# Tokens of experts 1 to 3: sixteen-bit halves transposed by DMA in place of TensorE transposes

## What is computed

```python
logits = flat_x @ Wg + bg                       # 2048 tokens, E = 4 experts
top_vals, top_idx = jax.lax.top_k(logits, 2)
probs = softmax(logits where chosen, -inf elsewhere)
for i in range(E):
    score = jnp.where(assigned, probs[:, i], -jnp.inf)
    sel_p, sel_idx = jax.lax.top_k(score, 512)  # capacity
    tok = flat_x[sel_idx]                       # 512 x 512
    h = jax.nn.gelu(tok @ W1[i])                # 512 x 2048
    y = h @ W2[i] * p                           # 512 x 512
    out = out.at[sel_idx].add(y)
```

## Time and profile before

| | |
|---|---|
| median of 3 runs | 478.77 us (478.63 to 479.13) |
| the profiled execution | 477.77 us, its span 476.0 us |
| mean granted clock of TensorE | 0.957 of full speed |
| busy PE, DVE, ACT, POOL | 414.5, 292.1, 313.1, 108.0 us |

### The profile page before, as it was taken

How to read it: one execution, slowest core, us unless ns; L and a number is a source line. 1 busy time by engine, 2 the same in 40 slices (tenths; PEclk the granted TensorE clock), 3 DMA queues, 4 the chain that set the end, 5 groups by cost and what they waited for, 6 DMA issues and landing times.

```text
span 476.0 us, 7146 instructions
## 1 busy us (share of the span) xinstructions
PE 414.5 (87%) x2039; PEld 201.4 (42%) x2039; DVE 292.1 (61%) x596; ACT 313.1 (66%) x487; POOL 108.0 (23%) x126
## 2 busy tenths in 40 slices
PE   2586877712899999999999999999999999999991
PEld 2343343401554444454444444444444444444440
DVE  7999999988499976564674155457514635560000
ACT  6798888998669773926778780577879147760000
POOL 0787746701300002521001311100041110001111
PEclk9999998955699999999999999999999999999997
DMA  7994120499400828438001925600092310001211
GB/s 265 341 351 180 44 90 1 161 343 360 129 2 0 349 91 291 109 74 326 0 0 61 372 52 196 204 0 1 11 374 79 42 24 0 0 0 9 36 22 22
DMA packets 23126, 59.64 MB, mean 125 GB/s; under 512 B 1280, under 2 KB 1408, under 8 KB 21056
## 3 DMA queue, kind: packets, MB, share of 16 engines
q1 hardware_dynamic: 19008, 50.17, 28.5%
q0 software_dynamic: 3664, 8.65, 9.0%
q10 hardware_dynamic: 432, 0.54, 0.3%
HBM read 46.78 MB, written 12.58 MB: 125 GB/s over the span
## 4 chain that ended last, share of the span: by engine, by line
PE 74%; DVE 15%; issue 3%; ACT 2%; POOL 2%; DMA 1%; ACTq 0%; DVEq 0%; POOLq 0%
PE ps L818 35%; PE ps L803 26%; PE ps L781 7%; DVE arena L1280 6%; PE ps L744 2%; DVE arena L1299 2%; DVE arena L1310 2%; PE ps L714 1%; DVE arena L1536 1%; DMA arena<-xn_table,idx 1%; PE ps L610 1%; ACT early L883 1%; POOL arena L1139 1%; PE ps L736 1%; DVE arena L1658 0%
## 5 line engine op out<-in xcount | busy, mean ns | idle before, releaser
L818 PE MATMUL ps<-arena 128*128 128x512 f16 x768 | 167.7, 379 | 0.0
L803 PE MATMUL ps<-arena,early 128*128 128x512 f16 x576 | 124.8, 379 | 0.0
L818 PEld LDWEIGHTS ps<-arena 128*128 128x128 f16 x768 | 74.6, 98 | 88.1
L803 PEld LDWEIGHTS ps<-arena,early 128*128 x576 | 56.3, 98 | 68.0
L1046 ACT ACTIVATE arena<-ps,up 128x512 f32<-128x512 f32 x64 | 43.8, 684 | 58.6 <-PE ps L803 40.0
L1709 DVE SCALAR_TENSOR_TENSOR arena<-arena,h_down 128x512 f32 x48 | 36.1, 751 | 58.9 <-ACT arena L1049 58.9
L1218 POOL DMA_INDIRECT result<-arena,idx x16 | 27.6, 1724 | 191.0 <-DVE arena L1737 137.8
L1049 ACT ACTIVATE arena<-arena,h_down 128x512 f32 x64 | 46.2, 721 | 8.7 <-ACT arena L1046 0.2
L1689 DVE SCALAR_TENSOR_TENSOR early<-w_raw,down,early 128x2048 f16<-128x2048 f32 x16 | 37.1, 2346 | 18.9 <-ACT early L1007 18.8
L1737 DVE TENSOR_SCALAR arena<-ps,yscale 128x512 f32<-128x512 f32 x16 | 12.0, 748 | 59.1 <-PE ps L818 49.1
L1052 ACT ACTIVATE arena<-rows,down x64 | 45.2, 706 | 0.0
(11 more groups left out here) (226 smaller groups left out, 461.2 us busy)
## 6 DMA issues: line engine op xcount, KB each, us to landing
w_raw<-in_L_ffn_W SPq DMA_DIRECT2D x4, 4096.0 KB, 13.9
rows<-in_L_ffn_W SPq DMA_DIRECT2D x3, 4096.0 KB, 17.6
rows<-in_L_ffn_W SPq DMA_DIRECT2D x4, 1024.0 KB, 9.2
result<-rows SPq DMA_DIRECT2D x3, 1024.0 KB, 6.8
early<-in_ctx SPq DMA_DIRECT2D x2, 1024.0 KB, 6.3
rows<-in_x SPq DMA_DIRECT2D x2, 1024.0 KB, 11.0
xn_table<-arena SPq DMA_DIRECT2D x4, 512.0 KB, 5.2
xn_table<-arena SPq DMA_DIRECT2D x2, 1024.0 KB, 4.8
```

The source lines that it names most:

```text
L803: last = nc.tensor.matmul(ps[:, PH[q], :], w[:, k, at], t[:, k, :], start=n == 0, stop=n == 3 * CT - 1)
L818: last = nc.tensor.matmul(ps[:, PY[s % 2], :], h[:, t, s * P:(s + 1) * P], w[:, t, :], start=t == 0 and n == 0, stop=t == HT - 1 and n == 2)
```

## The change

For experts 1 to 3 the tokens are split before they are transposed. ACT writes the high halves of a gathered piece as rows into a new buffer `tok_rows_hi` (which lies where `hot` lies). DVE writes the low halves as rows over the gathered piece itself (`tok_rows_lo` is a 16-bit view of `tok`). SP then issues, for each expert, four DMA transposes of 128 x 512 16-bit elements for the high and four for the low halves, from SBUF to SBUF, into `tok_hi` and `tok_lo`. A new semaphore, `c_across`, counts them (16 each). The up product of expert e waits for all eight of its own; so do the next `hot` table on DVE and the next gather on POOL.

```diff
+        tok_rows_lo = tok[:, :, :].rearrange("p s d -> p (s d)").bitcast(F16).rearrange("p (s d) -> p s d", s=ST)[:, :, 0:D]
+        tok_rows_hi = part(arena, [at[0]], (ST, D), F16)
...
-            with sp.Fori(1, E) as e:
+            for e in range(1, E):
...
+                for s in range(ST):
+                    sp.wait_ge(c_tokhi, START + e * CT + s + 1)
+                    sp.dma_start_transpose(tok_hi[:, :, s * P:(s + 1) * P], tok_rows_hi[:, s, :]).then_inc(c_across, 16)
+                for s in range(ST):
+                    sp.wait_ge(c_toklo, START + e * CT + s + 1)
+                    sp.dma_start_transpose(tok_lo[:, :, s * P:(s + 1) * P], tok_rows_lo[:, s, :]).then_inc(c_across, 16)
...
-                for k in blocks:
-                    for s in range(ST):
-                        last = nc.tensor.transpose(ps[:, PT[k], s * P:(s + 1) * P], tok[:, s, k * P:(k + 1) * P], ident)
-                    last.then_inc(c_tokt, 1)
...
                 pe.wait_ge(c_w1hi, START + (e + 1) * CT)
+                pe.wait_ge(c_across, e * 2 * ST * 16)
...
-                            if q == 0:
-                                pe.wait_ge(c_tokhi, START + e * CT + k + 1)
-                                pe.wait_ge(c_toklo, START + e * CT + k + 1)
...
-                down_block(e, 0)
-                down_block(e, 1)
-                tokens(e + 1, (0, 1))
-                down_block(e, 2)
-                tokens(e + 1, (2, 3))
-                down_block(e, 3)
+                for s in range(ST):
+                    down_block(e, s)
...
-            down_block(0, 3, {5: lambda: tokens(1, range(CT))})
+            down_block(0, 3)
...
+            def high_rows(done):
+
+                for s in range(ST):
+                    act.wait_ge(c_tok[s], (done + 1) * 16)
+                    hold(act, "act")
+                    nc.scalar.copy(tok_rows_hi[:, s, :], tok[:, s, :]).then_inc(c_tokhi, 1)
...
                 w1_high(e + 1)
+                high_rows(e + 1)
                 w2_magnitudes(e + 1)
-                token_high(e + 1)
...
-                pool.wait_ge(c_tokt, START + (e + 1) * CT)
+                if e == 0:
+                    pool.wait_ge(c_tokt, START + CT)
+                else:
+                    pool.wait_ge(c_across, e * 2 * ST * 16)
...
+            def token_low(done):
+
+                for s in range(ST):
+                    dve.wait_ge(c_tokhi, START + done * CT + s + 1)
+                    nc.vector.tensor_tensor(tok_rows_lo[:, s, :], tok[:, s, :], tok_rows_hi[:, s, :], ALU.subtract).then_inc(c_toklo, 1)
...
             take_y(0, 2)
-            w1_low(1, (2,))
-            token_low(1, range(CT))
-            w1_low(1, (3,))
+            token_low(1)
+            w1_low(1, (2, 3))
...
                 take_y(e, 1)
-                token_low(e + 1, (0, 1))
+                token_low(e + 1)
                 w1_low(e + 1, (2, 3))
                 take_y(e, 2)
-                token_low(e + 1, (2, 3))
```

More of the change, by code:

```diff
@@ L381, in program @@
         b_shift = sem("shifted_ready")
-        b_rsum = sem("softmax_sum_ready")
         b_wide = sem("wide_probs_ready")
@@ L417, in program @@
         c_none = sem("unneeded_rows_landed")
-        c_zero = sem("unneeded_index_set")
         c_tokt = sem("tokens_transposed")
@@ L421, in program @@
         c_toklo = sem("token_lo_ready")
+        c_across = sem("token_halves_transposed")
         c_wtop = sem("weight_top_ready")
@@ L430, in program @@
         c_wpow2 = sem("weight_power_bounded")
-        c_wpow3 = sem("weight_power_inverted")
         c_down = sem("weight_scale_ready")
@@ L549, in _ @@
             first_w2(3, (4,))
-            with sp.Fori(1, E) as e:
+            for e in range(1, E):
                 sp.wait_ge(c_w1hi, START + e * CT)
                 sp.wait_ge(c_w1lo, START + e * CT)
-                sp.dma_start(w1_raw[:, :, :], w1_v[:, bass.ds(e, 1)].rearrange("p a k h -> p (a k) h")).then_inc(s_w1, 16)
+                sp.dma_start(w1_raw[:, :, :], w1_v[:, e]).then_inc(s_w1, 16)
                 sp.wait_ge(c_w2hi, START + e * HT)
                 sp.wait_ge(c_w2lo, START + e * HT)
-                sp.dma_start(w2_raw[:, :, :], w2_v[:, bass.ds(e, 1)].rearrange("p a t d -> p (a t) d")).then_inc(s_w2, 16)
+                sp.dma_start(w2_raw[:, :, :], w2_v[:, e]).then_inc(s_w2, 16)
+                for s in range(ST):
[4 more added lines that the diff above has]
+                    sp.dma_start_transpose(tok_lo[:, :, s * P:(s + 1) * P], tok_rows_lo[:, s, :]).then_inc(c_across, 16)
         @block.tensor
@@ L704, in next_list @@
                 last.then_inc(b_hotused, 1)
-            def tokens(done, blocks):
-                for s in range(ST):
-                    pe.wait_ge(c_tok[s], (done + 1) * 16)
-                pe.wait_ge(b_taken, done * 2 + 2)
-                for k in blocks:
-                    for s in range(ST):
-                        last = nc.tensor.transpose(ps[:, PT[k], s * P:(s + 1) * P], tok[:, s, k * P:(k + 1) * P], ident)
-                    last.then_inc(c_tokt, 1)
             def keep_warm(count):
@@ L1039, in gelu_and_w2 @@
                 act.wait_ge(c_hsc, START + 2 * e + 2)
+                hold(act, "act")
+                act.wait_ge(c_w2sum, START + e * CT + CT)
                 hold(act, "act")
@@ L1230, in _ @@
                 pool.wait_ge(s_x1st[g], 16)
-            nc.gpsimd.memset(none[:, :], 0).then_inc(c_zero, 1)
-            pool.wait_ge(c_zero, 1)
+            nc.gpsimd.memset(none[:, :], 0).then_inc(s_mhalf, 1)
+            pool.wait_ge(s_mhalf, 3)
             nc.gpsimd.indirect_dma_start(tok[:, ST - 1, :], None, xn2_table, bass.IndirectOffsetOnAxis(ap=none[:, 0:1], axis=0),
@@ L1452, in _ @@
             step(nc.vector.tensor_reduce(psum_r[:, :], pex[:, :, :], AX.X, ALU.add))
-            nc.vector.reciprocal(psum_r[:, :], psum_r[:, :]).then_inc(b_rsum, 1)
-            dve.wait_ge(b_rsum, 1)
+            step(nc.vector.reciprocal(psum_r[:, :], psum_r[:, :]))
             for n in range(2):
@@ L1482, in scales_of @@
                 dve.wait_ge(c_wpow2, START + count)
-                nc.vector.tensor_copy(up[:, m:m + 1], wpow[:, m:m + 1]).then_inc(c_wpow3, 1)
+                nc.vector.tensor_copy(up[:, m:m + 1], wpow[:, m:m + 1])
                 nc.vector.reciprocal(down[:, m:m + 1], wpow[:, m:m + 1]).then_inc(c_down, 1)
@@ L1804, in _ @@
                 halves_of_h_and_w2(e, 0, 2)
+                dve.wait_ge(c_across, e * 2 * ST * 16)
+                hold(dve, "dve")
                 slots(e + 1)
```

## The result

The changed kernel takes 473.12 us in the median of 6 runs (472.65 to 475.01), beside 478.70 us for the kernel before (6 runs, 477.75 to 479.13). The ratio is 0.989, with a 95% interval of 0.987 to 0.991. The sum of the prediction gave 473.5 us.

The account below looks back on a forecast made before the run. TensorE's solid chain was taken to bound the kernel; removing 48 transposes takes off 5.23 us, with the DMA transposes hidden at no cost: 478.77 - 5.23 = 473.54 us on the median. The range was 472.5 to 491 us.

Parts of the forecast that it names:

- Which engine bounds: From 205 to 466.26 us the chain is TensorE alone, so a microsecond leaving TensorE there leaves the time.
- The size of the gain: Taking 48 transposes off TensorE's chain, 1.75 + 4 x 0.87 us, gains 5.23 us at most.
- When the rows are ready: Expert 1's high rows from ACT ready at 196.8 to 200.7 us, low ones from DVE at 202.7 to 204.9.
- The price c: Time by which one DMA transpose follows another in a train on SP's queue: 1.36 us.
- The landing of the last: Expert 1's last transpose, started at 206.8 us, lands 3.9 us later at 210.7, 0.8 us ahead of need.
- nothing exposed: The new wait before the up products costs nothing, hidden by down block 3; hidden or under 1.5 us exposed, chance 0.57.
- The third: Rival: each 128x128 block in a transfer pays on its own, c 5.3 us or more; about 549 us, chance 0.13.
- the first two rivals: Ahead of up products: partly hidden, 474.8 to 476.5 us, chance 0.13; transposes one after another, 490 or 507 us, chance 0.12.
- the clock's part: After a long stall TensorE's granted clock drops to 0.50 and recovers, losing 1.3 us.
- a pace of 2.5 us: Second rival's deciding point: expert 1 5.3 us late, experts 2 and 3 in time, no change; around it, chance 0.05.
- What was costed at nothing: Dropped up product waits, SP's written-out loop and regrouped semaphores sit where nothing is late: zero; transposes' new wait hidden: nothing.
- ACT's later magnitudes: On ACT, W2's magnitudes end 4 to 5 us later, at 208.2 us, before DVE wants them at 209.5: nothing shifts.

Follow-up runs that it names:

- the wide transposes: Changed kernel with an expert's four high transposes of 128 x 512 made two of 128 x 1024, low ones unchanged: 472.91 us, 0.988 of the kernel before.
- the late train: Changed kernel, but SP waits for all four low pieces of an expert before issuing the first of its eight transposes: 482.78 us, 1.010 of before.
- the small edits: Kernel before with only the SP loop written out and three semaphores dropped or regrouped: 478.61 us beside 478.05, ratio 1.0007.
- the halved transposes: Changed kernel with each DMA transpose cut into two of 128 x 256 elements, 16 for an expert: 489.35 us, 1.024 of before.

## Why the prediction was right

**Which engine bounds.** Right, and shown: what leaves TensorE's chain leaves the time, and what is added to it is added to the time (doubled transposes, 5.6 us).

**The size of the gain.** 5.23 us forecast, 5.6 measured in the medians (an interval of 4.2 to 6.0), 5.24 in the two traces on the stretch that the change touches. The traces are the firmer check: 5.6 and 5.23 differ by less than the interval.

**When the rows are ready.** Within 0.9 us: the first high rows at 197.5 (forecast: 196.8, in a profile that ran 0.94 us later), the fourth low piece at 205.3 (204.9). ACT's copies were 0.62 us long rather than 0.72, DVE's four from SBUF 2.48 us, as from PSUM, where I had allowed 2.9. That the transfers would have the DMA engines almost to themselves held only in part: in 276 to 284 us of expert 2 their share was 0.49, but in 200 to 210 us of expert 1 it was 0.82 to 1.24.

**The price c.** 1.36 us was taken from the gathers on POOL's queue; 1.3 was measured. The number was right by luck: I took it as the pace of independent transfers, from the gathers' issue on POOL, and it is the issue of a transposing instruction on SP, the same for 64 to 256 KB, while a load costs SP 0.37 us. The landing of the last, 3.9 us forecast, was 2.6, with 5.0 and 3.9 just ahead of it. So expert 1 had 2.1 us of room in place of 0.8, or 1.4 with the 0.75 us from the landing to the first matmul, which the forecast left out. The term that counted, nothing exposed, was right; it was right by 1.4 us.

**The rivals.** None of them took place. The third, a price for each 128x128 block, is ruled out by size: two, four and eight blocks take 1.24, 1.26 and 1.3 us. The Trainium skill's 1309 ns in "VectorE: DVE Perf Modes", "The three transpose paths", is for one block of 128x128. No run here has a transpose of one block alone, but instructions of two, four and eight blocks take no more than that of the queue, so multiplying it by the blocks gave a price that these runs don't bear out. By the 261 GB/s of the Trainium skill's page "DMA: Bandwidth & Descriptors", "Latency and other measured facts", a transpose would take 0.5 us by estimate. The pace was 1.3 us, set by the issue, and in the windows of the wide transposes the engines, with shares of 0.96 and 1.12, moved 181 and 211 GB/s, a fifth to a third less. What I held against the change besides, that a transpose costs TensorE only 0.109 us, did not count: it is 0.109 us of the engine that bounds the time, against 1.3 us for each transfer on a queue and on engines that had room. The place of the first two rivals was right, as the trains made longer show: the wait ahead of the up product is where a late train appears, first on expert 1. Their price per stall was too low. I put the clock's part at 1.3 us; it was 1.8 to 2.6 us after stalls of 2.8 us and more (and 0.2 us after those of 1.6 us and less). So at a pace of 2.5 us the change would, by estimate, have lost and not broken even: with a stall of 7.0 us, the late train was 4.7 us slower than the kernel before, where 7.0 - 5.2 gives 1.8.

**What was costed at nothing.** Confirmed for the small edits (ratio 1.0007) and for the DMA traffic (473.38 and 473.40 us). ACT's later magnitudes show nowhere in the chain. They end at 209.2 us, and expert 1's first gelu, which the changed kernel makes wait for them, starts at 215.18 and was released by TensorE.

## What to carry to other kernels

When one engine's chain is solid, work moved from it to DMA engines with room gained all of its pipelined time (here 0.109 us per transpose, not the 0.27 us that one lasts), as long as the train was done ahead of the point that needs it. Price such a train by instructions, not by bytes, up to the 256 KB tried here: number times 1.3 us, one landing (2.4 to 5.0 us, the longer ones beside other transfers), and the time from the landing to the first matmul, which was 0.75 to 0.81 us into this loop and 0.14 us where a plain matmul waited. Keep large loads behind it on its queue. Count more for a stall of TensorE than its length: those of 2.8 to 14.4 us here cost 1.8 to 2.6 us of clock besides, those of 1.6 us and less 0.2.

## What the runs showed of the hardware that I had not expected

- A transposing DMA from SBUF to SBUF holds SP for 1.24 to 1.3 us in the median whether it moves 64, 128 or 256 KB; single ones took up to 2.3 us. A 4 MB load takes 0.37 us, and 0.53 where it stood right behind a train.
- It moves small packets. SP's queue before and with the halved transposes:

```profile
q1 hardware_dynamic: 19008, 50.17, 28.5%
...
q1 hardware_dynamic: 32832, 53.33, 31.0%
```

  With the change it has 32064 - 19008 = 13056 more packets than before, 544 for each of the 24 transposes of 128 KB. With each cut in two there are 32832 - 32064 = 768 more: 32 for each added instruction. By estimate, then, 512 packets of 256 bytes carry the data, and 32 come with each instruction.
- Behind a 4 MB load on the same queue, the second transpose took 8.66 us to issue for expert 1 and 8.15 us for expert 2.
- After an idle time of 2.8 us on TensorE (expert 2 of the halved transposes) the up product took as much longer, 1.9 us, as after one of 8.0 us (1.8). After 1.6 us (expert 3 of the same kernel) it was 0.17 us longer.
